# GpSimd's gather loop written out over resident index lists, one wait per group of eight gathers

## The reference

```python
total_edge = concatenate([node_feats[src], node_feats[dst], edge_feats], axis=-1)
nbr_filter = sigmoid(_bn(total_edge @ W1.T + b1, g1, bt1))
nbr_core = softplus(_bn(nbr_filter, g2, bt2))
agg = segment_sum(nbr_filter * nbr_core, dst, num_segments=N_NODES)
new_node = _bn(agg, g3, bt3)
return _layernorm(x + node_feats + new_node)
```

## Time and profile before

| | us |
|---|---|
| median of 3 runs | 2782.18 |
| lowest and highest run | 2775.23, 2789.22 |
| span of the profiled execution | 2780.2 |
| first stage in it, to the last statistics of z | 2279.5 |
| GpSimd busy in the whole span | 1741.3 |

### The profile page before, as it was taken

One profiled execution on the slowest core, in us unless ns is written; L12 is line 12 of the kernel. 1 busy time (PEld: TensorE's weight loads), 2 busy tenths in 40 slices (PEclk: granted clock), 3 DMA queues, 4 the chain that ended last, 5 costly groups with the idle time before them and its releaser, 6 DMA issues. The chain is left out here.

```text
span 2780.2 us, 20646 instructions
## 1 busy us (share of the span) xinstructions
PE 892.3 (32%) x5706; PEld 444.1 (16%) x5706; DVE 1045.5 (38%) x1647; ACT 549.3 (20%) x526; POOL 1741.3 (63%) x1674
## 2 busy tenths in 40 slices
PE   4232222222223222222222222222222220177776
PEld 3010000000001000000000000000000000177662
DVE  3142222223222321222222222222123239899997
ACT  1000000000000000000000000000000019799974
POOL 4746676666666666666666667666676651187763
PEclk8655555555555555555555555555555555599998
DMA  6454444344434443444344434455664349898942
GB/s 199 111 164 94 102 120 117 98 110 125 108 82 119 126 108 90 108 128 117 82 112 123 118 93 107 126 153 145 181 182 117 88 118 385 323 308 297 294 150 94
DMA packets 247377, 404.56 MB, mean 146 GB/s; under 512 B 66782, under 2 KB 132124, under 8 KB 234736
## 3 DMA queue, kind: packets, MB, share of 16 engines
q1 hardware_dynamic: 141417, 290.49, 34.5%
q0 software_dynamic: 50048, 51.30, 10.2%
q10 hardware_dynamic: 55819, 61.63, 6.7%
HBM read 295.52 MB, written 107.76 MB: 145 GB/s over the span
## 5 line engine op out<-in xcount | busy, mean ns | idle before, releaser
L399 POOL DMA_INDIRECT rows<-p_table,idx x1500 | 1418.4, 946 | 738.8 <-issue 460.1
L446 PE MATMUL z_ps<-into_z,with_w 128*64 128x512 f32 (+1 forms) x784 | 381.2, 1071 | 756.3 <-issue 459.4
L551 ACT ACTIVATE z_sb<-z_ps 128x512 f32<-128x512 f32 x196 | 116.7, 596 | 2042.4 <-remote 1237.2
L716 DVE TENSOR_TENSOR z_sb<-z_sb,xg_ps 128x512 f32<-128x512 f32 x144 | 98.5, 684 | 738.7 <-remote 472.5
L493 PE MATMUL xg_ps<-ident,rows 128*128 128x128 f32 x564 | 156.8, 433 | 629.7 <-DMA rows<-p_table,idx 420.5
L685 DVE TENSOR_TENSOR into_z<-d_in,node_ps 84x1024 f32<-84x1024 f32 x196 | 235.3, 1201 | 156.3 <-issue 79.8
L611 DVE COPY idx<-src_idx 128x16 int32 (+1 forms) x93 | 16.9, 183 | 669.0 <-remote 391.4
L1008 POOL TENSOR_TENSOR h_buf<-h_buf,s_all 128x1536 f32<-128x1536 f32 x66 | 223.6, 3434 | 59.2 <-ACT h_buf L979 59.2
L493 PEld LDWEIGHTS xg_ps<-ident,rows 128*128 128x128 f32 x564 | 100.6, 216 | 864.1 <-DMA rows<-p_table,idx 563.2
L446 PEld LDWEIGHTS z_ps<-into_z,with_w 128*64 128x64 f32 x784 | 58.6, 203 | 829.1 <-issue 676.1
L718 DVE BATCH_NORM_STATS2 stats<-z_sb 128x512 f32 (+1 forms) x196 | 135.7, 692 | 65.4 <-DVEq L713 37.2
(11 more groups left out here) (156 smaller groups left out, 738.0 us busy)
## 6 DMA issues: line engine op xcount, KB each, us to landing
s_all<-edge_mem SPq DMA_DIRECT2D x102, 768.0 KB, 7.5
d_in<-dst_f SPq DMA_DIRECT2D x97, 672.0 KB
edge_mem<-z_sb ACTq DMA_DIRECT2D x97, 512.0 KB
into_z<-e_main SPq DMA_DIRECT2D x98, 336.0 KB
near<-near_mem SPq DMA_DIRECT2D x65, 504.0 KB, 4.9
near_mem<-near_one SPq DMA_DIRECT2D x97, 336.0 KB
rows<-p_table,idx POOLq DMA_INDIRECT x1500
agg<-edge_mem SPq DMA_DIRECT2D x8, 768.0 KB
```

The costliest lines, as they stand in the source:

```text
L399: gp.indirect_dma_start(out=to[0:size.tile, t, h, :], out_offset=None, in_=table, in_offset=bass.IndirectOffsetOnAxis(ap=which, axis=0)).t ...
L446: mm = pe.matmul(to[h * F:(h + 1) * F, 0:w], which(h)[0:height], into_z[s][0:height, h, 0:w], start=first, stop=last)
L551: act.activation(z_sb[s][:, 0:size.half], z_ps[s % 2][:, 0:size.half], ACT.Copy).then_inc(e_copied, 1)
L716: v.tensor_tensor(z, z, xg_ps[s][:, part], ALU.add).then_inc(z_copied, 1)
```

## The change

GpSimd's loop is written out, and its gathers read `src_idx` (for the last group `src_idx_r`) directly. The copied lists, their semaphore `idx_ready`, and VectorE's copies are gone. GpSimd no longer waits once for a pair, but before each group of eight gathers for `z_ready >= g - 3`, that is, for group g - 4 (for groups 8 to 11, whose buffers were last used by groups 0 to 3, for group g - 8). A `sem_inc` on `bumps` per pair is gone, and the last group waits for `w_in2`, the load of `src_idx_r` at the start.

```diff
@@ GpSimd
-                def gather(j, g, s, size, table):
-
-                    first = isinstance(g, int) and g < 2 * S
-                    if s % 2 == 0 and not first:
-                        gp.wait_ge(idx_ready, j - 3 + (isinstance(j, int) and j == PAIRS_OF - 1))
-                        gp.wait_ge(z_ready, j * 2 - (6 if isinstance(g, int) and g < 3 * S else 2))
-                        gp.sem_inc(bumps, 1)
+                def gather(g, size, table):
+
+                    s = g % S
+                    if g >= 2 * S:
+                        gp.wait_ge(z_ready, g - (2 * S if g < 3 * S else S) + 1)
                     to, done = (rows_ahead[s], ahead[s]) if is_ahead(g) else (rows[s], gathered[s])
+                    lists = src_idx[:, g, :] if size is FULL else src_idx_r[:]
                     for t in range(size.tiles):
                         for h in range(2):
                             place = h * size.tiles + t
-                            which = src_idx[:, g, place:place + 1] if first else idx[s][0:size.tile, place:place + 1]
+                            which = lists[:, place:place + 1]
...
-                    gather(g // 2, g, g, FULL, x)
+                    gather(g, FULL, x)
                 gp.wait_ge(p_stored, 16 * BLOCKS)
-                for g in range(S, 3 * S):
-                    gather(g // 2, g, g % S, FULL, p_table)
-                with gp.Fori(3, R_TURN) as i:
-                    for s in range(S):
-                        gather(i * 2 + s // 2, i * S + s, s, FULL, p_table)
-                for g in range(R_TURN * S, GROUPS):
-                    gather(g // 2, g, g % S, FULL, p_table)
-                gather(GROUPS // 2, GROUPS, R_SLOT, RAGGED, p_table)
+                for g in range(S, GROUPS):
+                    gather(g, FULL, p_table)
+                gp.wait_ge(w_in2, (4 + S) * 16)
+                gather(GROUPS, RAGGED, p_table)
@@ VectorE
-                v.wait_ge(src_in, 16)
-                for j in range(2):
-                    indices(4 + j, j)
...
-                    if s % 2 == 1 and not (isinstance(g, int) and (g < 2 * S or g + S > GROUPS)):
-                        v.wait_ge(z_ready, g + 1)
-                        indices(turn * 2 + s // 2 + 2, s // 2)
```

More of the change, by code:

```diff
@@ L183, in build @@
             src_idx_r = sb("src_idx_r", [T_P, 2 * T_TILES], I32)
-            idx_pair = [sb(f"idx{s}", [P, 2, 2 * TILES], I32) for s in range(2)]
-            idx = [idx_pair[s // 2][:, s % 2] for s in range(S)]
             rows = [sb(f"rows{s}", [P, TILES, 2, F]) for s in range(S)]
@@ L255, in build @@
             z_stored = [sem(f"z_stored{s}") for s in range(2)]
-            idx_ready, turned, xg_ready, hot_ready = (
-                sem(n) for n in ("idx_ready", "turned", "xg_ready", "hot_ready"))
+            turned, xg_ready, hot_ready = (
+                sem(n) for n in ("turned", "xg_ready", "hot_ready"))
             z_ready, z_copied, z_counted = sem("z_ready"), sem("z_copied"), sem("z_counted")
```

## The result

The changed kernel took 2760.0 us (median of 4 runs, 2754.55 to 2760.65) against 2779.94 for the kernel before on the same chip (4 runs, 2775.23 to 2789.22): a ratio of 0.9915, 95% interval 0.9892 to 0.9938. It is faster by 0.85%, some 20 us, where I had forecast 71. The direction was right and the time lies in the range, but the term that should have made the gain gave nothing that the runs can show.

A forecast was written before the change was run, and what follows sets the result against it. GpSimd's gather pace, 11.45 us per group with its waits, was taken as the first stage's bound. From 2780.2 us, -66 (later condition) and -5 (start) gave 2709, stated as 2711 against the median; range 2614 to 2900.

The forecast's parts named there:

- The pace of GpSimd is the bound, one for one: First stage: it goes at GpSimd's 11.45 us per group, and the end moves one for one with that.
- I expect the lateness to stay: TensorE's signals to ScalarE and VectorE: still late after the change, since loop and copied lists do not cause it.
- The later condition: GpSimd's wait before even groups, for g - 4 instead of g - 3: 11.45 to 11.09 us per group, -66 us.
- the walk: One GpSimd cycle followed from its restart at 1022.82 us: 9 groups in 99.8 us, with two waits of 4.8.
- the waits only move: Rival for GpSimd's waits: its 12% idle share is needed anyway, 11.45 us per group, 2775 to 2785 us; chance 0.20.
- The start, -5: Group 12's wait, now for group 8 instead of 9: perhaps 5 of its 24.5 us go.
- The copies, the lists and the loop, 0 (loop -11 to +11): VectorE's index copies removed, lists read from src_idx, GpSimd's loop written out: each 0, the loop bounded -11 to +11 us.
- By it up to 16.9 us more would come off: VectorE's index copies: by the skill's rule they block GpSimd's descriptor writes, up to 16.9 us; the trace disagreed.
- Code fetched instead of a loop: GpSimd's written-out gathers: some 7 more instruction packets, +11 us if each stopped GpSimd 1.55 us; taken as 0.
- The slower rival, 0.30: Per-group waits of GpSimd close the gate again and signals never clear: 2870 or 2958, at worst 3395 us; chance 0.30.
- What the trace should show: Signs: no idle at L611, more VectorE idle before its add, some 41 GpSimd waits (195 us), consumers 8 us late.

The follow-up runs named there:

- e9: Changed kernel, but GpSimd again waits once per pair of groups, for group g - 3: 2756.82 us, ratio 0.9890 to the kernel before (2787.42).
- e7: Changed kernel with eight row buffers instead of four up to group 160: 2766.14 us, ratio 0.9921 to the kernel before.
- e8: Changed kernel with four gathers per group instead of eight from group 12 on, values wrong: 1767.4 us, ratio 0.6337 to the kernel before.
- e10: Changed kernel with four unused matmuls behind each TensorE window and each group's transposes: 2804.56 us, ratio 1.0063 to the kernel before.
- e12: Changed kernel with VectorE waiting for the gathers in TensorE's place and passing on one signal per group: 2764.03 us, ratio 0.9920 to the kernel before.
- e13: Changed kernel without SyncE's loads to d_in after the first: 2753.68 us, ratio 0.9883 to the kernel before.
- e16: Kernel before with only GpSimd's loop written out: 2465.05 us, ratio 1.0002 to the kernel before.
- e17: Kernel before with the loop written out and gathers reading src_idx, copies and old waits kept: 2465.06 us, ratio 0.9998 to the kernel before.
- e18: Kernel before with only GpSimd's loop written out, run once more: 2464.66 us, ratio 1.0002 to the kernel before.
- e2: Kernel before with only GpSimd's loop written out, first run: 2466.54 us, ratio 0.9999 to the kernel before (2466.46).

## Why the prediction came out as it did

*The pace of GpSimd is the bound, one for one.* Right: 182 x (11.41 - 11.31) = 18 of the spans' 21.8 us are the stage's pace.

*"I expect the lateness to stay."* Right, and it had nothing to do with loop or copies. It was read as the kernel's own, which it is only on a late chip.

*"The later condition", "the part that moves time", -66 us.* This is the step that failed: where I had put 66 us, nothing was measured. `e9`, without it, stands at 0.9890 beside 0.9915 and 0.9901 with it, and the waits are 278.8 us before and 280.0 after. In the walk I took group 89's signal at the pace before it, at 67.7, and so no wait at 70.1. But that signal had come 5.7 us after GpSimd stopped. With the stop moved, it moved too: in the profile after, GpSimd ran 56 gathers, ended the last at 69.6 after the restart (1061.39), and the signal came 5.8 us later (1067.18). The length of a pause (I took 4.8 us, they are 5.95 and 5.17) was nearly right; that a group could be won without paying it later was not. The cycle was 8 groups in 90.4 us, and not 9 in 99.8. The rival "the waits only move" had the mechanism right, an idle share of 12% that is due in any case, and I gave it 0.20. Its time, 2775 to 2785, was missed all the same, because it too left out the small gaps. That the measured time lies in my range, and on the side that I forecast, is luck: it got there by a term that I had at nothing.

*The start, -5.* Wrong: group 12 waited 24.2 us, where it had waited 24.46.

*The copies, the lists and the loop, 0 (loop -11 to +11).* Together they are where the 20 us come from. The interval of the first comparison is 17 to 30 us, and that of `e9` 21 to 40, against my bound of 11. More than half of the 21.8 us is the odd gaps. Within the groups from 12 on, the profile of before has eight of 1.85 us, the first two 96 and the others 192 gathers apart, 12.4 us over the usual 0.30. The eight written-out kernels on late chips (the changed one twice, `e7`, `e8`, `e9`, `e10`, `e12`, `e13`) have none over 0.46 us, and 0.0 to 1.9 us in all. The kernel before on a prompt chip, loop and all, has none either. So they come with the loop on a late chip. That the loop makes them, and not the copies and bumps that went with it, is argued: the loop alone was not taken out on a late chip. My lower bound of -11 was about their value, and I had taken 0. Some 9 us of the spans' difference are left, 4 of them the shorter gathers. Which of the parts carries the rest is open, since `e16`, `e17` and `e18` met prompt chips. That fewer instructions cost less on a late chip would agree with `e10`, where more cost more, but it is argued and not shown.

*"By it up to 16.9 us more would come off"*, the rule of the Trainium skill ("SBUF — State Buffer", section "SBUF: two separate sides") that VectorE's copies hold GpSimd's descriptor writes. On a prompt chip the copies' removal gave 1.0001 (0.9992 to 1.0010), so 2.0 us at the most. In the kernel before on a prompt chip 71 of the 94 copies began while a gather was being issued, and none of those gathers took over 947 ns. No run here shows the rule at these copies.

*Code fetched instead of a loop.* 11 more packets came (58 for 47) where I had some 7. My 222 per packet divided executed instructions, loop turns counted again and again, by packets fetched. On prompt chips no gap was longer for it: `e2`, `e16` and `e18` stand at 0.9999 to 1.0002.

*The slower rival, 0.30.* It did not occur: a wait per group closes the gate again only once per cycle, 8 gathers on, and its idle share is the same (11.7% of the pace, 12.3% before).

*What the trace should show.* No idle time at L611, VectorE's idle time before its add grown (738.7 to 1036.3 us), waits put down to TensorE or to none: right. 41 waits of 195 us in all, two per nine groups: it was 51 and 280.0, the start's 24.2 among them, two per eight. Consumers late by 8 us and more: 17 to 33 in the rows shown.

## What to carry to other kernels

If waits change their releaser and place with each edit and keep their sum (278.8, 280.0, 270.8 and 286.4 us in four kernels here), suspect the idle share of something that is full. Count what the stage puts through it, and change its number (half the gathers), its lead (twice the buffers) and who waits before a wait is moved. Before a wait that ends "remote" is taken for the kernel's own, count the trace's semaphore records and profile the unaltered kernel on another chip: here that one run would have told more than the whole walk.

## What the runs showed of the hardware

- The same program took 2464 to 2466 us on some chips and 2780 to 2787 on others, at the same granted clock (0.53 and 0.52 in the stage) and the same length of a gather (944 and 947 ns). While GpSimd issues indirect gathers densely, TensorE's signals arrive late on the latter, and ScalarE took a window up to 40 us after its end. No recorded signal of VectorE or ScalarE was over 0.02 us late there. Whether it is the chip or the occasion stays open.
- On a late chip a gather of 128 rows costs 1.35 us and a group's other work 0.51, by an estimate from two paces; on the others 8 gathers cost 8 x 1.25. What is full there, if something is, stays open: the completion of the gathers, their descriptors, the recording, something else. 64 rows per gather were to tell, and that run met a prompt chip.
- GpSimd's signal to itself can be late there by up to 1.9 us (a gap of 2.20 for 0.27).
- Traces from late chips hold a quarter of the semaphore records (9,757 to 11,658 for 40,123 to 41,763).
- On a prompt chip a gather of 64 rows costs 1.21 us, one of 128 rows 1.25.
- On a late chip the kernel with the loop had gaps of 1.85 us, mostly every 192 gathers; on a prompt chip it had none.
- No version that computes everything beat the changed kernel by more than the intervals (0.9884 to 1.0063 beside its 0.9901 and 0.9915 on late chips, 0.9998 to 1.0010 on prompt ones).
